# Two attention blocks in one program: the value product moved behind the first-query energies, two tiles for the last layer norm, and a new written-out order of steps

## What is computed

```python
def mha(x, kv, Wq, Wk, Wv, mask, causal):          # 16 heads of 8
    Q, K, V = (project(t, w) * mask for t, w in ((x, Wq), (kv, Wk), (kv, Wv)))
    energy  = Q @ K.T
    lengths = count(energy[first query] != 0)       # per head
    energy  = where(column >= lengths, -inf, energy)
    if causal: energy = where(column > row, -inf, energy)
    return (softmax(energy / sqrt(8)) @ V) * mask

# block 1
x1 = layernorm(x + mha(x, x, Wq1, Wk1, Wv1, mask0, True))              # "A"
x2 = layernorm(x1 + mha(x1, context, Wq2, Wk2, Wv2, mask1, False))     # "B"
x3 = layernorm(x2 + (relu(x2 @ fc1.T + b1) @ fc2.T + b2) * mask0)      # "B" too
# block 2: 16 heads of 64                                              # "C"
s   = (x3 @ wq + bq) @ (context @ wk + bk).T / 8 + 2 * f               # f: 32 x 16 x 64 x 64
out = layernorm(softmax(s) @ (context @ wv + bv) @ wo + bo + x3)
```

## Time and profile before

| | |
|---|---|
| median of three runs | 362.23 us (359.26, 362.23, 460.11) |
| the profiled execution | 360.42 us |
| its span, first to last instruction | 358.6 us |
| granted TensorE clock | 1.000 |
| instructions | 13324 |
| HBM read, written | 15.99 MB, 1.05 MB |
| loads of f, stores of the output | 16 each |

### The profile page before, as it was taken

One profiled execution on the slowest core, in us unless ns is written; L12 is line 12 of the kernel. 1 busy time (PEld: TensorE's weight loads), 2 busy tenths in 40 slices (PEclk: granted clock), 3 DMA queues, 4 the chain that ended last, 5 costly groups with the idle time before them and its releaser, 6 DMA issues.

```text
span 358.6 us, 13324 instructions
## 1 busy us (share of the span) xinstructions
PE 344.8 (96%) x5376; PEld 264.1 (74%) x5383; DVE 293.7 (82%) x836; ACT 241.1 (67%) x567; POOL 242.1 (68%) x376
## 2 busy tenths in 40 slices
...
DMA packets 13180, 17.88 MB, mean 50 GB/s; under 512 B 1600, under 2 KB 10176, under 8 KB 13120
## 3 DMA queue, kind: packets, MB, share of 16 engines
...
HBM read 15.99 MB, written 1.05 MB: 48 GB/s over the span
## 4 chain that ended last, share of the span: by engine, by line
PE 71%; DVE 11%; issue 4%; DMA 4%; ACT 4%; POOL 4%; SPq 3%; POOLq 0%; DVEq 0%
PE C_E L545 7%; PE C_E L600 5%; PE C_E L561 4%; PE B_E L407 4%; PE A_E L407 4%; PE C_E L590 4%; PE A_E L426 4%; PE B_E L329 3%; PE C_E L577 3%; PE B_E L426 3%; DMA out<-osb 3%; PE A_E L440 2%; PE B_E L440 2%; PE C_E L502 2%; PE C_E L521 2%
## 5 line engine op out<-in xcount | busy, mean ns | idle before, releaser
L1039 POOL TENSOR_TENSOR Sc<-Sc,C_mx 128x512 f32<-128x512 f32 x28 | 29.3, 1047 | 28.8 <-DVE C_mx L947 28.8
L989 POOL TENSOR_TENSOR A_kblk<-A_qk,cst 128x1024 f32<-128x1024 f32 x16 | 31.3, 1954 | 22.1 <-DVE A_qk L833 22.0
L731 ACT ACTIVATE qT<-C_E,bq 128x128 f32<-128x128 f32 x112 | 31.5, 374 | 10.7 <-PE C_E L545 10.6
L999 POOL TENSOR_TENSOR L_rstd<-L_ve,cst 128x1 f32<-128x1 f32 x64 | 35.2, 550 | 5.0
L1010 POOL TENSOR_TENSOR L_xg<-L_xh,vec_sb 128x128 f32<-128x128 f32 x64 | 30.2, 472 | 10.2 <-DVE L_xh L907 10.0
L989 POOL TENSOR_TENSOR B_kblk<-B_qk,cst 128x1024 f32<-128x1024 f32 x16 | 30.4, 1898 | 2.2 <-DVE B_qk L833 2.2
L1048 POOL TENSOR_TENSOR Pc<-Pc,C_rd 128x512 f32<-128x512 f32 x28 | 29.0, 1044 | 2.9 <-DVE C_rd L957 2.9
L545 PE MATMUL C_E<-x3T,wq_sb 128*128 128x128 f32 x224 | 30.5, 281 | 0.0
L997 POOL TENSOR_TENSOR L_ve<-L_mv,cst 128x1 f32<-128x1 f32 x64 | 12.3, 192 | 23.6 <-DVE L_mv L898 23.3
L545 PEld LDWEIGHTS C_E<-x3T,wq_sb 128*128 128x128 f32 x224 | 27.0, 192 | 1.6 <-issue 0.6
L600 PE MATMUL C_E<-wo_sb,C_zT 128*128 128x128 f32 x224 | 27.8, 277 | 0.1
...
## 6 DMA issues: line engine op xcount, KB each, us to landing
...
out<-osb SPq DMA_DIRECT2D x16, 64.0 KB, 1.5
...
```

The lines of the kernel that those rows point to most:

```text
L731: last = act.activation(place(n).qT[:, 4 * g + j], place(n).E[g][:, j * P:(j + 1) * P], ACT.Identity, bias=bq8[:, 4 * g + j:4 * g + j + 1] ...
L989: tt(a.kblk[:], a.qk[:, 1].unsqueeze(1).to_broadcast([P, 8, P]), at["rmask"].unsqueeze(2).to_broadcast([P, 8, P]), ALU.mult).then_inc(a.s_ ...
L999: tt(l.rstd[:], l.ve[:], at["power"], ALU.pow).then_inc(l.s_rstd, 1)
L1039: tt(v, v, place(n).mx[:, 8 * g:8 * g + 8].unsqueeze(2).to_broadcast([P, 8, S]), ALU.subtract).then_inc(C.s_sub, 1)
```

## The change

Three edits. First, the eight instructions of the product with Wv leave `X.qkv` and stand at the head of `X.e0`, behind its wait for `q0`; `s_qkv` is raised by the Wk product, and `B.xts`, which overwrites the input `xc` of that product, now waits for `s_e0`. Second, `osb` becomes two tiles with a semaphore each, so that `C.gb#n` waits for the store of pair n-2. Third, `PLAN` is a new order of the same 1920 steps.

```diff
-        osb = sb("osb", [P, D])
+        osb = [sb(f"osb{k}", [P, D]) for k in range(2)]
...
-        s_st = sem("s_stored")
+        s_st = [sem(f"s_stored{k}") for k in range(2)]
...
             def store(n):
                 sp.wait_ge(L4.s_out, n + 1)
-                sp.dma_start(out[n * P:(n + 1) * P, :], osb[:]).then_inc(s_st, 16)
+                sp.dma_start(out[n * P:(n + 1) * P, :], osb[n % 2][:]).then_inc(s_st[n % 2], 16)
...
                     mm(a.J[:, 0:P], wqk[0][:], xq, start=True, stop=True)
+                    mm(a.J[:, P:2 * P], wqk[1][:], xkv, start=True, stop=True).then_inc(a.s_qkv, 1)
+                return step
+
+            def e0(a, wv1):
+
+                def step(n):
+                    pe.wait_ge(a.s_q0, n + 1)
+                    xkv = cols(xTs, n) if a is A else xc[:, 1]
                     for b in range(2):
-
                         for r in range(2):
-                            last = mm(a.J[S * r:S * r + S, 2 * P + S * b:2 * P + S * b + S], xkv[:, S * b:S * b + S],
-                                      wqkv[2][:, S * r:S * r + S], start=True, stop=True)
-                    last.then_inc(a.s_qkv, 1)
...
+                            mm(a.J[S * r:S * r + S, 2 * P + S * b:2 * P + S * b + S], xkv[:, S * b:S * b + S],
+                               wv1[:, S * r:S * r + S], start=True, stop=True)
                     for b in range(2):
                         last = mm(a.J[S * b:S * b + S, 0:H], a.qk[:, 1, S * b:S * b + S], a.q0[:, b], start=True,
                                   stop=True)
...
                 if n:
-                    act.wait_ge(Bc.s_qkv, n)
+                    act.wait_ge(Bc.s_e0, n)
...
-            def gb(l, out_of, *free):
+            def gb(l, out_of, *free, stored=False):
...
+                    if stored and n > 1:
+                        pool.wait_ge(s_st[n % 2], 16 * (n // 2))
...
-                     "C.gb": gb(L4, lambda n: osb[:], (s_st, 16, 1))}
+                     "C.gb": gb(L4, lambda n: osb[n % 2][:], stored=True)}
...
 PLAN = """
-A.qkv#0 A.qk#0 A.q0#0 A.e0#0 A.nz#0 A.cnt#0 K.warm#0 A.cut#0 A.v#0 K.warm#1 A.kblk#0 A.qkv#1 A.e#0 K.warm#2
...
+K.warm#0 A.qkv#0 K.warm#1 A.qk#0 A.q0#0 A.e0#0 A.nz#0 A.cnt#0 K.warm#2 A.cut#0 A.v#0 K.warm#3 A.kblk#0
...
```

More of the change, by code:

```diff
@@ L347, in bvo, with qkv @@
                 last.then_inc(bvo_ready, 1)
-            def qkv(a, wqkv):
+            def qkv(a, wqk):
                 def step(n):
@@ L1066 @@
 PLAN = """
[L1067 to L1086, removed]
@@ L1222 @@
[L1222 to L1224 removed]
+K.warm#0 A.qkv#0 K.warm#1 A.qk#0 A.q0#0 A.e0#0 A.nz#0 A.cnt#0 K.warm#2 A.cut#0 A.v#0 K.warm#3 A.kblk#0
+K.warm#4 A.qkv#1 K.warm#5 A.e#0 C.chi#0 K.warm#6 A.max_0#0 A.qk#1 K.warm#7 C.clo#0 A.q0#1 A.sub_0#0 K.warm#8
+A.e0#1 A.max_1#0 A.exp_0#0 K.warm#9 C.whi#0 A.sub_1#0 K.warm#10 A.m0#0 A.pt_0#0 A.exp_1#0 A.nz#1 A.pts_0#0
@@ new lines @@
+B.max_1#6 C.e#4 A.pts_0#8 A.nz#9 C.gb#1 B.f1s#5 A.exp_1#8 A.cnt#9 B.f2#5 C.fadd_0#4 B.pt_0#6 C.store#1 B.f2s#5
+C.fadd_1#4 A.pt_1#8 B.pts_0#6 B.f3#5 C.max_0#4 C.o#3 A.pts_1#8 B.y3#5 C.sub_0#4 B.am#7 B.3st#5 B.cm#7
+C.exp_0#4 C.xh#2 A.pv_0#8 B.3rstd#5 C.y#3 A.pv_1#8 B.sub_1#6 C.k_0#8 A.zts#8 B.3xh#5 B.exp_1#6 C.max_1#4
+C.k_1#8 B.3gb#5 C.ks_0#8 A.cut#9 B.pt_1#6 C.ks_1#8 C.den_0#4 B.tr#7 A.kblk#9 C.v_0#5 B.pts_1#6 A.v#9 B.xts#7
+C.v_1#5 C.vs_0#5 A.m0#12 A.z#8 C.vs_1#5 B.pv_0#6 C.sub_1#4 A.zn#8 B.pv_1#6 C.x3t#5 B.zts#6 B.qkv#7 A.y#8
@@ new lines @@
+C.sub_1#6 C.exp_0#6 B.f3#7 C.y#5 B.e#8 A.pts_1#10 B.y3#7 C.exp_1#6 B.3st#7 C.k_0#10 B.max_0#8 B.3rstd#7
+C.k_1#10 B.sub_0#8 C.ks_0#10 C.x3c#6 B.3xh#7 A.kblk#11 A.pv_1#10 B.exp_0#8 B.max_1#8 C.v_0#7 C.ks_1#10 C.st#5
+B.tr#9 A.zts#10 B.sub_1#8 C.v_1#7 C.vs_0#7 B.3gb#7 C.den_0#6 B.xts#9 B.pt_0#8 B.exp_1#8 B.qkv#9 C.den_1#6
+C.vs_1#7 C.nrm_0#6 A.z#10 B.qk#9 B.pt_1#8 B.pts_0#8 B.q0#9 C.x3t#7 A.zn#10 B.e0#9 C.nrm_1#6 B.pts_1#8 A.y#10
+C.x3ts#7 B.pv_0#8 B.nz#9 C.chi#12 B.pv_1#8 A.st#10 B.cnt#9 C.q_0#7 B.zts#8 B.cut#9 A.rstd#10 A.v#11 C.q_1#7
@@ new lines @@
+B.am#10 C.store#5 C.sub_0#7 B.f3#8 C.y#6 B.pt_1#9 B.cm#10 C.loadf#7 B.y3#8 C.k_0#11 A.pts_1#11 B.pts_1#9
+B.3st#8 C.k_1#11 C.max_1#7 C.ks_0#11 B.3rstd#8 B.pv_0#9 A.cut#12 C.exp_0#7 B.pv_1#9 C.sub_1#7 A.pv_0#11
+B.3xh#8 B.zts#9 A.pv_1#11 C.den_0#7 C.ks_1#11 B.tr#10 C.v_0#8 C.x3c#7 B.xts#10 A.v#12 B.3gb#8 A.zts#11
+B.qkv#10 C.st#6 C.vs_0#8 C.v_1#8 A.kblk#12 B.qk#10 B.q0#10 A.z#11 C.vs_1#8 B.e0#10 A.zn#11 C.exp_1#7 C.x3t#8
+B.z#9 A.y#11 C.x3ts#8 B.nz#10 A.qkv#13 C.nrm_0#7 A.st#11 C.q_0#8 C.den_1#7 A.rstd#11 C.q_1#8 B.zn#9 C.qs_0#8
```

293 lines of the change are left out of this document (145 added, 148 removed).

## The result

The changed kernel takes 350.78 us (median of 4 runs, 349.91 to 350.82) against 361.7 for the kernel before: ratio 0.971, 95% interval 0.966 to 0.977. One of the four runs before took 460.11 us and is left out of the ratio. The profiled execution took 350.75 us, its span 349.0.

A forecast was written before the change was run, and what follows sets the result against it. Bound: PE's list in the middle, latency at both ends, two late stores between. Terms -3.4 + 0.3 + 2.0 - 1.0 - 0.5 + 0 = -2.6 us against the profiled 360.42 gave 357.8 us; 8-in-10 range 352.5 to 362.5.

The forecast's parts named there:

- the price of the product with Wv: Eight instructions moved on PE from X.qkv to X.e0: 0.38 us each step, nothing removed; +0.3 us (0 to 12.2).
- the start: PE's work up to C.x3t#0 and just behind: moved zero products and real work filling gaps, -1.0 us (-4 to +2.5).
- the end: B.e#15 goes ahead of B.f1#14 and C.v#13, up to 1.66 us sooner; -0.5 us (-1.7 to +1).
- the cover of pairs 7 and 11: Less work ahead of C.zt in two pairs: another 0.26 us lost in pair 7, 0.5 us paid in pair 11.
- The second tile: C.gb no longer waits for the store just before, removing two late-store delays; -3.4 us (-2.8 to -5.9).
- The cover of C.zt: Shorter A.qkv leaves PE waiting before C.zt, 0.32 us in pairs 0, 1, 2 and 6; in sum +2.0 (0 to +3.7).
- No wait for a store: Sign in the profile after: POOL has no wait for a store, or only short ones.
- C.zt of #7 to #9 about 19.8 apart: Sign in the profile after: C.zt starts of pairs 7, 8 and 9 stand about 19.8 us apart.
- PE's wait in front of the product with Wv: Sign at L379: no more idle time than now; a sum over 2 us would make the prediction wrong.
- the second rival: Product with Wv loses its cover, X.e0 holds PE, 0.38 us idle per step; 365 us with 20 of 32; chance 0.15.
- Tighter order: Rival: PE's order is packed tighter than visible, 0.35 us less in each of 14 pairs; 353 us, chance 0.22.
- the late stores: Rival: store#9 behind two loads of f delays C.gb#11, the second tile's gain is gone; 361 us, chance 0.10.

The follow-up runs named there:

- e0: Not a run: a step of the kernel's order, A.e0 or B.e0, PE's first-query energies behind q0; it has no measured time of its own as a kernel.
- e4: The changed kernel with one osb tile again, its stores back in rising order; 351.25 us, ratio 0.9741 to the kernel before.
- f3: The changed kernel with C.zt of pairs #0, #1, #2, #6, #7 and #10 put behind a later step; 358.77 us, ratio 0.9951.
- f5: The changed kernel with all 16 K.warm steps (zero products) left out; 351.44 us, ratio 0.9738.
- e8: The changed code with the old order up to C.x3t#11 and the new order behind it; 361.41 us, ratio 1.0023.
- f2: The kernel before, in its old order, with the second tile and the moved product with Wv together; 360.98 us, ratio 1.0001.

## Why the prediction was wrong

**The step that failed is the price of the product with Wv.** "Their count and shape don't change, so nothing is removed; what changes is what they cover" took the 0.38 us of the earlier trace rows as a property of the eight instructions. It is a property of their neighbours: 0.38 us with other shapes on both sides, 0.28 with their own behind; and the product with Wk in front of them takes 0.32 instead of 0.22. In sum they cost 0.47 us a step in X.qkv and 0.23 in X.e0. The timeline from which the earlier trace rows are taken has the starts of Wq and Wk just ahead of them; I didn't compare these with each other, and did not ask what the tiling rule makes of full and tiled products side by side. The second part of the step is "what they cover": the prediction counted the cover that is lost at C.zt, and put at nothing, without a look, what the products would cover in their new place. There they fill idle time of PE behind X.e0. The term was +0.3 (0 to +12.2), "nothing" its lower end; it measured -8.8 in the new order, of which some 7 are shapes, and +1.4 to +3.3 in the old. Excluding a gain there was the mistake, and with it the range.

**Two terms were not additive.** The whole order by itself gives -1.1, near what the start, the end and the cover of pairs 7 and 11 add up to (about -0.7; the rest of the cover term goes with the move). With the move it gives 362.8 - 351.25 = 11.5 us. The order was summed as if each step kept its length.

**The second tile** was right in mechanism and size, -3.1 for -3.4, when it is the only edit. In the new order it is worth 0.5: in e4, with one tile, POOL waits for a store once, for 2.2 us, where it waited for 5.9 in four places before. So -3.4 was in the sum where -0.5 belongs.

**The cover of C.zt** (+2.0) was right as a wait: 0.27 and 0.28 us in pairs #7 and #6 for 0.26 and 0.32, 2.1 us in 6 places in all, 0.7 of which is pair 10's of before. The 0.5 us of pair 11 didn't come. As a cost it is less clear: taking the waits away as in f3 costs more than they do.

**The start** (-1.0, with -4 as its lower end) measured -3.4; C.x3t#0 starts at 56.30 us, not 59.48. The announced sign was 1 us. The working leaned on the zero products, which f5 shows to be worth some 0.7 us; of PE's 1.57 us of gaps in the second stretch 0.65 was filled (18.43 to 19.08), with 22 more instructions.

**The end** isn't separated: e8, with the new tail alone, is 0.4 us above f2, inside the measurement.

**The signs.** No wait for a store: so. C.zt of #7 to #9 about 19.8 apart: 19.6 and 18.9. The pace of the first six pairs is 19.52, within the 0.3 that was allowed, while the forecast was wrong, so that bound was too wide: 0.25 us a pair is 4 us. PE's wait in front of the product with Wv sums to 2.3 us, over the 2 that was named, but the loss that it was to announce (the second rival) didn't come; 1.3 of it is a single place.

**The rivals.** "Tighter order", 353, came nearest in number. Its reason, the weight loads' 74%, isn't what the runs show: that share is still 74%, and the list itself became shorter. The lost cover of the product with Wv and the late stores did not happen.
